# A fused attention-pooling and gated-MLP kernel: bias rows on another DMA queue, two staging regions for the transposes, and a planner with new costs and due times

## The reference

```python
h = tanh(xn @ W1.T + b1);  s = h @ w2 + b2            # one score for each token
e = exp(s - max over the sequence)
ctx = cumsum(e * xn) / cumsum(e)                      # running weighted mean over tokens
attn = tanh(concat(ctx, xn) @ Wc.T + bc)              # Wc: 256 x 512
gate = xn @ (w_gate / 127).T;  up = xn @ (w_up / 127).T   # int weights, 768 x 256
ffn = (silu(gate) * up) @ (w_down / 127).T            # 256 x 768
out = x + attn + ffn
```

## Time and profile before

| | before |
|---|---|
| median of 3 runs | 399.25 us |
| the profiled execution's own time | 399.43 us |
| its span, first to last instruction | 397.2 us |
| TensorE matmul busy | 388.1 us (98%) |
| VectorE busy | 297.0 us (75%) |
| ScalarE busy | 249.8 us (63%) |
| GpSimd busy | 199.7 us (50%) |

### The profile page before, as it was taken

How to read it: one execution, slowest core, us unless ns; L and a number is a source line. 1 busy time by engine, 2 the same in 40 slices (tenths; PEclk the granted TensorE clock), 3 DMA queues, 4 the chain that set the end, 5 groups by cost and what they waited for, 6 DMA issues and landing times.

```text
span 397.2 us, 7879 instructions
## 1 busy us (share of the span) xinstructions
PE 388.1 (98%) x2735; PEld 269.9 (68%) x2735; DVE 297.0 (75%) x632; ACT 249.8 (63%) x467; POOL 199.7 (50%) x259
## 2 busy tenths in 40 slices
PE   6999999999999999999999999999999999999996
PEld 4667576666666588576686876767758677685765
DVE  5699999999898778886866846689766776745361
ACT  3797898789898646974736574556353644627250
POOL 1545522543636799999733130699834664502000
PEclk9999999999999999999999999999999999999999
DMA  8999233032317028656611001433422130100001
GB/s 270 354 349 259 54 42 67 7 75 56 79 28 165 28 65 130 144 139 108 125 36 54 26 28 52 112 107 81 101 85 54 53 108 2 53 28 28 28 27 60
DMA packets 54718, 36.44 MB, mean 92 GB/s; under 512 B 31759, under 2 KB 50064, under 8 KB 54672
## 3 DMA queue, kind: packets, MB, share of 16 engines
q1 hardware_dynamic: 54320, 35.60, 35.8%
q10 hardware_dynamic: 288, 0.26, 0.2%
q0 software_dynamic: 64, 0.00, 0.0%
HBM read 20.06 MB, written 8.45 MB: 72 GB/s over the span
## 4 chain that ended last, share of the span: by engine, by line
PE 76%; POOL 10%; issue 5%; DVE 4%; DMA 3%; ACT 1%; SPq 1%; POOLq 0%; ACTq 0%; DVEq 0%
PE bank L680 33%; PE bank L716 33%; PE bank L736 7%; POOL ex L1209 3%; DMA xt<-xt 2%; POOL xt L1217 2%; POOL wide L1231 2%; DVE stats L936 1%; DVE bank L1101 1%; DMA sg<-in_w2b 1%; PE bank L1346 1%; POOL ex L1214 1%; PE bank L673 1%; SPq L1260 1%; DVE wide L1106 0%
## 5 line engine op out<-in xcount | busy, mean ns | idle before, releaser
L716 PE MATMUL bank<-xt,narrow 128*128 128x512 f16 x768 | 177.3, 379 | 0.4 <-issue 0.4
L716 PEld LDWEIGHTS bank<-xt,narrow 128*128 128x128 f16 x768 | 75.0, 98 | 76.2 <-issue 0.6
L680 PE MATMUL bank<-narrow,wide 128*128 128x256 f16 x792 | 96.4, 273 | 0.0
L680 PE MATMUL bank<-narrow,xt 128*128 128x256 f16 x768 | 93.7, 274 | 1.9 <-ACT bank L814 1.7
L680 PEld LDWEIGHTS bank<-narrow,xt 128*128 128x128 f16 x768 | 74.7, 98 | 21.0 <-ACT bank L814 3.3
L680 PEld LDWEIGHTS bank<-narrow,wide 128*128 128x128 f16 x792 | 77.4, 98 | 9.5
L1101 DVE SCALAR_TENSOR_TENSOR bank<-bank,sg 128x512 f32<-128x512 f32 x96 | 65.6, 693 | 17.9 <-PE bank L716 15.3
L861 ACT ACTIVATE sg<-bank 128x512 f32<-128x512 f32 x96 | 56.6, 593 | 33.0 <-PE bank L716 31.6
L1106 DVE TENSOR_TENSOR wide<-bank,wide 128x512 f16<-128x512 f32 x90 | 60.7, 681 | 19.8 <-ACT wide L868 18.4
L868 ACT ACTIVATE wide<-bank 128x512 f16<-128x512 f32 x90 | 53.1, 593 | 34.4 <-DVE bank L1101 34.1
L1231 POOL TENSOR_TENSOR wide<-ex,wide 128x512 f16<-128x512 f32 x32 | 39.4, 1242 | 69.8 <-ACT wide L882 69.8
(11 more groups left out here) (103 smaller groups left out, 267.1 us busy)
## 6 DMA issues: line engine op xcount, KB each, us to landing
rows<-scratch SPq DMA_DIRECT2D x16, 512.0 KB, 5.1
out_y<-xres SPq DMA_DIRECT2D x31, 256.0 KB, 2.2
xres<-in_x SPq DMA_DIRECT2D x15, 512.0 KB, 8.8
xt<-xt SPq DMA_TRANSPOSE x56, 2.5
wide<-in_wg SPq DMA_DIRECT2D x1, 768.0 KB, 6.8
wide<-in_wu SPq DMA_DIRECT2D x1, 768.0 KB, 9.2
wide<-in_wd SPq DMA_DIRECT2D x1, 768.0 KB, 10.9
wide<-in_wc SPq DMA_DIRECT2D x1, 512.0 KB, 11.6
```

The lines of the kernel that those rows point to most:

```text
L680: return pe.matmul(dst, lhs, rhs, start=False, stop=stop, skip_group_check=True)
L716: mm = pe.matmul(b[:, :], pg.up(which, k, j), pg.xn(sx, k, tok), start=n == 0, stop=n == len(todo) - 1)
```

## The change

Five things. **(1)** The row of b1 and the row of w2 are loaded by ScalarE's queue, behind its two tiles of x; GpSimd's queue loads nothing. **(2)** TensorE spreads only these two (two products, four matmuls); bc and b2 are broadcast to all partitions by two DMAs at the end of SyncE's loads, with semaphores of their own, and the step Ec is gone. The warm-ups are nine in a row ahead of the spreading, none behind it. **(3)** `waiting` has two regions by turns: the columns of block 15 for odd blocks, of block 13 for even ones. Xh of block i waits for the transposes of block i - 2. Tx of block 13 waits for those of block 12, Tx of block 15 for those of 13 and 14. The four semaphores of the tiles are doubled, a set for even and a set for odd blocks. **(4)** The planner's costs of B, R, Sv, Sc, N, Xm and the branch of TensorE are raised. **(5)** C of block i is due at 38.0 + 3.7 i, and Ln, Xh, Xm and Tx of blocks 2 and up are due 3 us earlier.

```diff
-    "B": (VE, 0.95, 1.05), "R": (VE, 0.8, 0.9), ... "Sv": (VE, 0.75, 0.85),
+    "B": (VE, 0.97, 1.07), "R": (VE, 0.84, 0.94), ... "Sv": (VE, 0.78, 0.88),
-    "Sc": (VE, 1.85, 1.95), ... "N": (PO, 2.95, 3.05), ... "Xm": (PO, 1.2, 1.3),
+    "Sc": (VE, 2.0, 2.1), ... "N": (PO, 3.2, 3.3), ... "Xm": (PO, 1.5, 1.6),
-    "BrT": (TE, 0.2, 0.2), ...
+    "BrT": (TE, 0.6, 0.6), ...
...
+def waits_as(i):
+    if i == LAST:
+        return LAST - 1
+    return i - 2 if FIRST_T + 2 <= i < SPARE_TO else None
...
-        ctx = 34.0 + 4.0 * i if i < LAST else NBLK * KH
+        ctx = 38.0 + 3.7 * i if i < LAST else NBLK * KH
...
-                due["Ln", i, pr] = due["S", i, pr] - 8.7 - early(i)
-                due["Tx", i, pr], due["Xm", i, pr] = due["S", i, pr] - 5.5 - early(i), due["S", i, pr] - 7.0 - early(i)
-            due["Xh", i, pr] = due["S", i, pr] - 7.6 - early(i) if i >= FIRST_T else end["Lb", i, pr] + 0.1
+                due["Ln", i, pr] = due["S", i, pr] - 11.7 - early(i)
+                due["Tx", i, pr], due["Xm", i, pr] = due["S", i, pr] - 8.5 - early(i), due["S", i, pr] - 10.0 - early(i)
+            due["Xh", i, pr] = due["S", i, pr] - 10.6 - early(i) if i >= FIRST_T else end["Lb", i, pr] + 0.1
...
-        return [(("Ln", i, x), 0), *([(("Tx", i - 1, x), 0)] if i > FIRST_T else []),
+        return [(("Ln", i, x), 0), *([(("Tx", waits_as(i), x), 0)] if waits_as(i) else []),
...
-        return [(("Xm", i, x), 0), *([(("Tx", i, 0), 4.7)] if x else []), *([(("Tx", LAST - 1, 1), 0)] if i == LAST else [])]
+        return [(("Xm", i, x), 0), *([(("Tx", i, 0), 4.7)] if x else []), *([(("Tx", i - 1, 1), 0)] if i in (LAST - 2, LAST) else [])]
...
-            b = LAST if i < SPARE_TO else 0
+            b = LAST - 2 * (i % 2 == 0) if i < SPARE_TO else 0
...
-                if i > FIRST_T:
-                    for s, count in pg.x_ready(i - 1, n):
+                if waits_as(i) is not None:
+                    for s, count in pg.x_ready(waits_as(i), n):
                         act.wait_ge(s, count)
...
-                if (i, n) == (LAST, 0):
-                    for t in range(4):
-                        sp.wait_ge(s_t[t], 16 * (LAST - FIRST_T))
+                if n == 0 and i in (LAST - 2, LAST):
+                    for s, count in [*pg.x_ready(i - 1, 0), *pg.x_ready(i - 1, 1)]:
+                        sp.wait_ge(s, count)
+                    if i == LAST:
+                        for s, count in [*pg.x_ready(i - 2, 0), *pg.x_ready(i - 2, 1)]:
+                            sp.wait_ge(s, count)
...
+            sp.dma_start(bc_every, biases[D:].partition_broadcast(P)).then_inc(s_bc, 16)
+            sp.dma_start(b2b, w2b2_in[D:].partition_broadcast(P)).then_inc(s_b2, 16)
...
             load_first(act, 3)
+            act.dma_start(b_row, biases[0:D].rearrange("(o d) -> o d", o=1)).then_inc(s_b, 16)
+            act.dma_start(w2_row, w2b2_in[0:D].rearrange("(o d) -> o d", o=1)).then_inc(s_w2, 16)
...
-            for n in WARM:
-                warm_up(n)
+            for n in range(WARM):
+                mm = pe.matmul(bank[n % BANKS][:, :], warm[:, 0:P], warm[:, 0:BLK], start=True, stop=True)
+            mm.then_inc(p_warm, 1)
             pe.wait_ge(v_set, 3)
             pe.wait_ge(s_b, 16)
             pe.wait_ge(s_w2, 16)
-            to_every(bank[BANKS - 1], 0, b_row[:, 0:D])
-            to_every(bank[BANKS - 1], D, w2_row[:, 0:D]).then_inc(p_b, 1)
-            to_every(bank[BANKS - 2], 0, b_row[:, D:])
-            to_every(bank[BANKS - 2], D, w2_row[:, D:]).then_inc(p_b, 1)
-            for n in WARM_REST:
-                mm = warm_up(n)
-            mm.then_inc(p_warm, 1)
+            to_every(bank[BANKS - 1], 0, b_row)
+            to_every(bank[BANKS - 1], D, w2_row).then_inc(p_b, 1)
...
-            pool.dma_start(b_row, biases.rearrange("(o d) -> o d", o=1)).then_inc(s_b, 16)
-            pool.dma_start(w2_row, w2b2_in.rearrange("(o d) -> o d", o=1)).then_inc(s_w2, 16)
```

More of the change, by code:

```diff
@@ L202, in due_times @@
             due["Ch", i, k], due["Cl", i, k] = ctx - 10.0 + 2.4 * k, ctx - 9.3 + 2.4 * k
-    for st, t in {"W1h": -4, "Ea": -4.5, "Tb": end["S", 0, 0] - 0.4, "Ec": end["S", 0, 0], "W1l": -3, "K1": 40, "Wgh": -4, "Wuh": -2, "Wdh": 3, "Kg": 41, "Kh": 43, "Ku": 45, "Kx": 46, "Kd": 47, "Ke": 48, "Ky": 50,
+    for st, t in {"W1h": -4, "Ea": -4.5, "Tb": end["S", 0, 0] - 0.4, "W1l": -3, "K1": 40, "Wgh": -4, "Wuh": -2, "Wdh": 3, "Kg": 41, "Kh": 43, "Ku": 45, "Kx": 46, "Kd": 47, "Ke": 48, "Ky": 50,
                   "Kc": 42, "Kf": 55, "Kp": 58, "Fl": 58, "Wch": 60, "Wcl": 61, "BrT": 60, "BrS": 60, "BrV": 60,
@@ L221, in needs @@
     m = KH * i + x
-    if kind in ("W1h", "Wgh", "Ea", "Ec"):
+    if kind in ("W1h", "Wgh", "Ea"):
         return []
@@ L340, in __init__ @@
         self.whole = {n: not wide and n < BANKS - 1 for n in range(BANKS)}
-        self.open_now, self.freed = set(), {n: 7.0 if n >= BANKS - 2 else 0.0 for n in range(BANKS)}
+        self.open_now, self.freed = set(), {n: 7.0 if n == BANKS - 1 else 0.0 for n in range(BANKS)}
         self.behind, self.freed_behind = set(), set()
@@ L512, in block_kernel @@
         s_w1, s_wc, s_wg, s_wu, s_wd, s_tri = map(sem, ("s_w1", "s_wc", "s_wg", "s_wu", "s_wd", "s_tri"))
-        s_b, s_w2, s_ident, s_out, s_er, s_again = map(sem, ("s_b", "s_w2", "s_ident", "s_out", "s_er", "s_again"))
+        s_b, s_w2, s_bc, s_b2, s_ident, s_out, s_er, s_again = map(sem, ("s_b", "s_w2", "s_bc", "s_b2", "s_ident", "s_out", "s_er", "s_again"))
         a_32, v_32, g_32 = map(sem, ("a_32", "v_32", "g_32"))
-        s_t = [sem(f"s_t{t}") for t in range(4)]
+        s_t = [[sem(f"s_t{odd}_{t}") for t in range(4)] for odd in range(2)]
         s_rows = [sem(f"s_rows{n}") for n in range(2)]
@@ L531, in block_kernel @@
         A_W, V_W, G_W = 2, 2, 3
-        WARM = (6, 0, 1, 2, 3)
-        WARM_REST = (4, 5)
+        WARM = 9
         def half(t):
@@ L624, in x_ready @@
                     return [(v_xlo, self.nth("Xl", i, pr))]
-                return [(s_t[t], 16 * (i - FIRST_T + 1)) for t in (2 * pr, 2 * pr + 1)]
+                return [(s_t[i % 2][t], 16 * ((i - FIRST_T) // 2 + 1)) for t in (2 * pr, 2 * pr + 1)]
             def h_ready(self, i, j):
@@ L659, in open_bank @@
                 eng.wait_ge(*pg.freed(last))
-            elif pg.plan.place[kind, i, n] >= BANKS - 2:
-                eng.wait_ge(a_b, BANKS - pg.plan.place[kind, i, n])
+            elif pg.plan.place[kind, i, n] == BANKS - 1:
+                eng.wait_ge(a_b, 1)
             return bank_of(pg, kind, i, n)
@@ L869, in scalar_step @@
             elif kind == "Cs":
-                act.wait_ge(a_b, 2)
+                act.wait_ge(s_bc, 16)
                 bias_seed(act, pg, 1, open_bank(act, pg, "C", i, n), a_cs, len(tiles_of(i, n)))
@@ L882, in scalar_step @@
                 act.activation(pg.ctx(0, i, n, slice(0, BLK)), ex[:, i % EX_RING, n, :], ACT.Copy).then_inc(a_c, 1)
-            elif kind in ("Ea", "Ec"):
-                first, at = (0, BANKS - 1) if kind == "Ea" else (2 * D, BANKS - 2)
-                last = 2 * D if kind == "Ea" else 3 * D + 1
-                act.wait_ge(p_b, 1 if kind == "Ea" else 2)
-                act.activation(every[:, first:last], bank[at][:, 0:last - first], ACT.Copy).then_inc(a_b, 1)
+            elif kind == "Ea":
+                act.wait_ge(p_b, 1)
+                act.activation(every[:, 0:2 * D], bank[BANKS - 1][:, :], ACT.Copy).then_inc(a_b, 1)
             elif kind == "Tb":
@@ L1260, in sync_step @@
                     sp.dma_start_transpose(xt16[:, :, :, lo:lo + P].rearrange("p s k t -> p (s k) t"),
-                                           waiting(i, n)[:, t % 2, :]).then_inc(s_t[t], 16)
+                                           waiting(i, n)[:, t % 2, :]).then_inc(s_t[i % 2][t], 16)
             elif kind == "Er":
@@ L1347, in to_every @@
                                  skip_group_check=True)
-            def warm_up(n):
-                return pe.matmul(bank[n][:, :], warm[:, 0:P], warm[:, 0:BLK], start=True, stop=True)
-            for n in WARM:
-                warm_up(n)
+            for n in range(WARM):
+                mm = pe.matmul(bank[n % BANKS][:, :], warm[:, 0:P], warm[:, 0:BLK], start=True, stop=True)
+            mm.then_inc(p_warm, 1)
             pe.wait_ge(v_set, 3)
```

18 lines of the change are left out of this document (9 added, 9 removed).

## The result

The changed kernel takes 396.95 us (median of 9, 396.08 to 397.55) against 400.14 us for the kernel before (9 runs together with new ones, 398.62 to 401.67): the ratio is 0.992, 95% interval 0.9899 to 0.9941. The profiled executions are 397.04 and 399.43 us, 2.39 us apart, and it is these 2.39 us that the views can account for. The total lies in the forecast's range (393.0 to 398.0), 2.15 us above the forecast's 394.8.

What follows compares the result with a forecast made beforehand. TensorE, its matmuls covering 98% of the span, was taken to bound the kernel; 2.3 us from the start plus 2.3 from the late starts made 4.6 off the profiled 399.43: 394.8 us, range 393.0 to 398.0.

Steps and rivals of the forecast that it cites:

- the prediction's own test: Wrong if TensorE's late starts from 22 us to the end total above 2 us, or a single one exceeds 1 us.
- Loads, warm-ups, spreading, first sums: Start: row lands by 5.4 us, warm-ups issue until 5.37, four spreading matmuls, scores start at 9.0 to 9.7 us.
- The level during the scores: TensorE's clock in block 0's 24 score matmuls: gain 0.7 us if it rises late, 2.6 if early; 2.3 taken.
- Rival 1: Start: clock still low at the scores, so the start gives 0.7 to 1.0 us; total 396.3 us; chance 0.17.
- The cover of the start: 22 to 66 us: VectorE must also come 2.3 us early; if not, 0.5 to 1 us of the start's gain goes.
- bc and b2 by broadcast: SyncE's queue: two more issues, 128 KB, read far later; costs nothing because DMA has room from 22 us on.
- Two regions: Staging of blocks 4 to 13: removes shorter ScalarE waits that TensorE does not show; block 15's 5.04 us wait stays.
- Costs: 127 to 194 us: longer planned costs, with the due times, remove 2.3 of 2.8 us of TensorE's late starts.
- Due times: 127 to 194 us: later C unloads GpSimd, at 92%, and earlier staging puts transposes ahead; shares the 2.3 us gain.
- rival 2: Whole order: late starts come up elsewhere, 2.3 us from the start and 0 from the order; 397.1 us; chance 0.15.
- Rival 3: 22 to 66 us: VectorE binds, so the start gives only 1.1 us; total 396.0 us; chance 0.08.
- Rival 4: Block 13: Ln waits on ScalarE for block 1's C; a 12 us wait costs 8, total 403.8 us; chance 0.05.

Runs made afterwards that it cites:

- The start alone: The kernel before with only the new row loads, nine warm-ups, two rows spread and two broadcasts; 399.71 us, ratio 0.9994.
- the loads spread: The changed kernel with x loads of blocks 10 to 12 behind block 2's transposes and 13 to 15 behind block 5's; 395.25 us, ratio 0.990.
- more warm-ups: The changed kernel with seven more 512-column warm-up matmuls, four behind the spreading, three between transposes and first scores; 397.75 us, ratio 0.995.
- The VectorE costs alone: The kernel before with only the planner's costs of B, R, Sv, Sc and TensorE's branch raised, GpSimd's as before; 398.46 us, ratio 0.9966.

## Why the prediction came out as it did

*The total.* 4.6 us were forecast and 2.39 measured between the profiled executions (3.2 between the medians). The time is in the range and the sign is right, but the sum was made of one term that was too small and one that should have been nothing. By the prediction's own test (after 22 us a single late start above 1 us, or more than 2 us in all) it was wrong in a step: there are two, of 1.60 and 0.54 us. That the time came into the range even so is in part luck: the start gave nothing where 2.3 us were summed, and the late region gave 0.8 more than its term.

*Loads, warm-ups, spreading, first sums.* The nine warm-ups went without a gap to 5.4 us, the spreading began at 5.48, the copy Ea at 6.98 (forecast 6.75 or 7.43) and the scores at 9.21 (forecast 9.0 to 9.7). These steps were right.

*The level during the scores.* "I take 2.3, near the high end" failed. The level did rise early, and it fell again: the prediction asked only whether it would rise. Only four spreading products and eight short transposes, with idle time between them, stood before the fall; in the profile with seven more full-height matmuls in those places it held. Why it held is less sure than that: of the three profiles with the seven, two rose late (10.6 and 13.4 us) and had no early rise to lose; of the four with nine warm-ups alone, all rose between 5.2 and 6.2 us and fell again. The start gave 0.94 us, not 2.3. Rival 1 named this size, with a late rise for its cause; its 0.8 us was right, its cause was not, in this execution.

*The cover of the start.* This is the step that failed in kind. The prediction looked for what could take the gain back in VectorE, and put DMA aside ("DMA has room from 22 us on", by the share of 0.64). That share is a mean over 22 to 66 us. In its first 13 us DMA is at 1.10, and block 2's transposes stand behind 13 loads in one queue. The start alone gave 0.9994: the true term was 0, and the wait even took 0.55 us more than the start had given. With the loads spread, the start's 1.1 us did last.

*bc and b2 by broadcast.* Costed at nothing because DMA has room. The two issues do stand ahead of all 13 loads, and the scores of block 2 start 0.77 us later than before. Most of that is not theirs: the start alone has the same two issues and starts these scores only 0.15 us later than before (38.93), and the due times alone, without them, 1.13 later (39.91). What goes with it is how much DMA had moved by then. From 0 to 20 us it is 312 GB/s in the kernel before, 311 in the start alone and with more warm-ups (39.12), but 299 in the changed kernel and 302 with the due times alone. Why DMA differs is open.

*Two regions.* Nothing forecast, nothing measured (1.0019). The reason given, that the 5.04 us wait is block 15's on block 14 and stays, holds: with the whole change ScalarE still waits there, only shorter, as the line that answers to 185.38 in the earlier trace rows shows:

```profile
184.93 0.63 ACT L848 ACTIVATE xt<-xt 128x512 f16<-128x512 f32 x1 [1.95 <-DMA xt<-xt]
```

*Costs.* Mis-sized: 2.3 of 2.8 us forecast, 3.08 measured. The late starts in the earlier trace rows all went, and the change of costs alone does it. The reason given, costs that were too short, is right for Xm and wrong for N. N was judged by its mean over all blocks, 2.89 us in the earlier trace rows, and by a guess of more where both engines are loaded. Here are N's two operations and Xm, GpSimd between 127 and 194 us in the kernel before:

```profile
L1209 POOL TENSOR_TENSOR ex<-xt 128x512 f32<-128x512 f16 x13 | 18.7, 1435 | 0.1
L1214 POOL TENSOR_TENSOR ex<-ex,rows 128x512 f32<-128x512 f32 x13 | 16.5, 1269 | 1.0
...
L1217 POOL TENSOR_TENSOR xt<-xnat,xt 128x512 f16<-128x512 f32 x4 | 8.3, 2076 | 0.0
L1217 POOL TENSOR_TENSOR xt<-xt 128x512 f16<-128x512 f32 x5 | 6.8, 1364 | 1.3 <-ACT xt L842 1.3
```

Xm, the last two lines, took 2.08 us in five of nine cases (the first line's four and one of the second's) where 1.2 were planned, 1.68 in the mean. N took 1.435 + 1.269 = 2.70 us, already less than its old cost of 2.95; the new 3.2 is further off. And with the new order the durations are others again, the same stretch of the changed kernel:

```profile
L1221 POOL TENSOR_TENSOR xt<-xnat,xt 128x512 f16<-128x512 f32 x4 | 4.6, 1151 | 0.0
```

So it is shown that an order made with the higher costs has no late start there; that it is so because the costs are nearer to the truth is not. The VectorE costs alone remove most of the late starts too.

*Due times.* "C starting later unloads GpSimd" was no cause of the gain: due times alone gave 0.9999. The changed kernel's GpSimd is indeed less busy there (56.56 us), but the gain is there without it.

*The rivals.* New stalls for old, rival 2, is what the parts tried alone show: under the old costs of GpSimd and another order, late starts of 0.2 to 1.8 us come up at places between 39 and 187 us. Rival 3 did not happen. Rival 4 did not either: Ln of block 13 had no such wait.

## What to carry to other kernels

A gain at the start counts only if the first thing fixed from outside, here the landing of a queue of loads, does not stand in its way: before counting such a gain, look for the first wait on a DMA behind the start, and what is ahead of that DMA on its queue. When the loads are moved, look at the next transfer that they will stand ahead of. And when the order of work comes from a planner, look at each step's duration in the stretch in which it is tight, not at the mean over the kernel; but the durations change with the order, so try the planner's costs by themselves and judge them by the late starts that the new order leaves.

## What the runs showed of the hardware

The granted clock fell again while TensorE still had work. In the changed kernel it rose between 5.5 and 6.4 us (the spreading takes 1.47 us instead of 2.07), TensorE then had one idle stretch of 0.74 us and one of 0.46 with eight matmuls of 128 columns between them, and it fell at about 9.6 us, in the first scores; 16 of them went at 0.213 us each. The Trainium skill ("TensorE: Matmul & The Clock Gate", Part 1, What's actually happening) says that the moment of a rise depends on where the first matmul falls in a window that does not start with the kernel; the seven profiles with one and the same nine warm-ups agree, with a rise anywhere from 4.2 to 13.4 us and the spreading at 1.10 to 2.07 us. The table of the Trainium skill in that section names an idle array for the fall; here the array was not idle throughout.

A DMA transpose that lands in a median of 2.5 us took up to 7.3 us behind loads in the same queue. With no load issued close before them, in two runs, all four of block 2 took 2.5 to 2.6.

One and the same GpSimd operation takes 1.16 or 2.08 us. In the kernel before, between 127 and 194 us, all of Xm's long ones have 1.12 us of VectorE's scan beside them, but so has one of the short ones nearly (1.08); for example:

```profile
153.15 1.16 POOL L1231 TENSOR_TENSOR wide<-ex,wide 128x512 f16<-128x512 f32 x1
153.36 2.02 DVE L1124 TENSOR_TENSOR_SCAN ex<-rows,ex 128x512 f32<-128x512 f32 x1
154.26 2.08 POOL L1217 TENSOR_TENSOR xt<-xnat,xt 128x512 f16<-128x512 f32 x1
156.31 1.15 POOL L1209 TENSOR_TENSOR ex<-xt 128x512 f32<-128x512 f16 x1
```

GpSimd's spans are rough in these traces, and the cause was not tried by a run. The Trainium skill ("SBUF — State Buffer", SBUF: two separate sides) has a rule that would do this: VectorE and GpSimd share a pair of ports; whichever comes first, a VectorE instruction with two inputs in SBUF or a GpSimd instruction that reads SBUF, holds the pair to its end, and the other waits in full. The rows above agree with it; the rule would also explain why one planned cost for Xm or N cannot be right in every stretch.
